# A fused macaron block on one core: scores 12 steps ahead of the exponentials instead of 15, maxima split and loaded at steps 4 and 5 of a unit

## What is computed

```python
x = x + 0.5 * ffn(layernorm(x))
x = x + attn(layernorm(x))
x = x + 0.5 * ffn(layernorm(x))
# ffn(x) = mxfp4(x) @ mxfp4(weight).T + bias: blocks of 32 values are scaled and rounded to 4-bit floats
# attn: q, k, v projections with bias, rotary embedding of q and k, 16 heads of 8 values,
#       softmax(q k^T / sqrt(8)) v over 512 positions
```

## Time and profile before

| | us |
|---|---|
| median of 3 runs | 617.38 |
| lowest and highest | 612.36 and 617.54 |
| the profiled execution | 620.8 |
| its span, first to last instruction | 618.9 |
| mean granted TensorE clock | 0.944 |

### The profile page before, as it was taken

How to read it: one execution, slowest core, us unless ns; L and a number is a source line. 1 busy time by engine, 2 the same in 40 slices (tenths; PEclk the granted TensorE clock), 3 DMA queues, 4 the chain that set the end, 5 groups by cost and what they waited for, 6 DMA issues and landing times.

```text
span 618.9 us, 10478 instructions
## 1 busy us (share of the span) xinstructions
PE 517.9 (84%) x2724; PEld 177.0 (29%) x2724; DVE 452.4 (73%) x1037; ACT 393.2 (64%) x773; POOL 250.7 (41%) x452
## 2 busy tenths in 40 slices
PE   0453999799979998999889897999889995999862
PEld 0121233233323332333223232333323331322211
DVE  6674879587988797768957598869957784788214
ACT  8343149386958684678837585768747683667750
POOL 6010266215753665345723465346723543011300
PEclk9999999799999998899979899999969996999995
DMA  5016102600161015100350015100440026000000
GB/s 159 1 34 143 27 3 53 153 2 1 35 146 27 20 36 128 45 19 11 92 107 19 6 35 131 44 18 19 96 96 19 2 59 147 13 9 1 6 14 17
DMA packets 21685, 30.84 MB, mean 50 GB/s; under 512 B 4333, under 2 KB 19321, under 8 KB 19321
## 3 DMA queue, kind: packets, MB, share of 16 engines
q1 hardware_dynamic: 21624, 30.13, 20.3%
HBM read 21.34 MB, written 8.39 MB: 48 GB/s over the span
## 4 chain that ended last, share of the span: by engine, by line
PE 54%; DMA 11%; DVE 9%; POOL 8%; issue 7%; ACT 6%; SPq 4%; POOLq 0%; ACTq 0%; DVEq 0%
PE sc L1120 15%; PE ot L1133 14%; PE st L1109 12%; DMA feat_k<-parts_k 8%; PE misc L1074 4%; DMA parts_k<-qkparts_k 3%; SPq L333 3%; DVE negmax L908 2%; ACT probs L639 2%; PE misc L1055 2%; PE misc L1098 2%; POOL rstd_f L404 2%; SPq L335 1%; PE misc L1073 1%; POOL qkparts_k L496 1%
## 5 line engine op out<-in xcount | busy, mean ns | idle before, releaser
L908 DVE TENSOR_REDUCE negmax<-sc 128x1 f32<-128x512 f32 x512 | 331.9, 681 | 106.6 <-PE sc L1120 106.2
L639 ACT ACTIVATE probs<-st 128x512 f32<-128x512 f32 x512 | 273.4, 606 | 127.1 <-PE st L1109 126.4
L1120 PE MATMUL sc<-feat_k,feat_q 96*128 96x512 bf16 x512 | 197.8, 411 | 38.6 <-DMA feat_k<-parts_k 23.9
L1109 PE MATMUL st<-feat_q,feat_k 99*128 99x512 bf16 x512 | 162.1, 395 | 2.9 <-ACT probs L639 2.2
L1133 PE MATMUL ot<-probs,vfeat 128*32 128x512 f32 x1024 | 143.2, 634 | 1.0 <-ACT probs L639 1.0
L1120 PEld LDWEIGHTS sc<-feat_k,feat_q 96*128 96x128 bf16 x512 | 51.2, 100 | 208.7 <-DVE negmax L908 127.4
L1109 PEld LDWEIGHTS st<-feat_q,feat_k 99*128 99x128 bf16 x512 | 50.7, 100 | 71.2 <-ACT probs L639 38.8
L467 POOL TENSOR_TENSOR cosd<-qkv,rope 128x256 f32<-128x256 f32 x28 | 20.4, 728 | 57.6 <-ACT qkv L602 57.5
L404 POOL TENSOR_TENSOR rstd_pj<-ve_pj,nhalf 128x4 f32<-128x4 f32 x8 | 8.3, 1038 | 75.2 <-DVE nm_pj L779 75.2
L446 POOL TENSOR_SCALAR maxparts<-negmax 128x16 bf16<-128x16 f32 x32 | 8.3, 258 | 67.9 <-DVE negmax L908 67.9
L1040 PE MATMUL misc<-identb,xq_f 128*128 128x128 bf16 x64 | 6.9, 236 | 28.9 <-DVE xq_f L842 28.3
(11 more groups left out here) (143 smaller groups left out, 529.0 us busy)
## 6 DMA issues: line engine op xcount, KB each, us to landing
feat_q<-parts_q SPq DMA_DIRECT2D x48, 192.0 KB
feat_k<-parts_k SPq DMA_DIRECT2D x48, 192.0 KB
parts_q<-qkparts_q SPq DMA_DIRECT2D x24, 128.0 KB, 2.3
parts_k<-qkparts_k SPq DMA_DIRECT2D x24, 128.0 KB, 2.3
xres<-in_L_attn_x_dram SPq DMA_DIRECT2D x8, 256.0 KB, 5.1
out_dram<-xres SPq DMA_DIRECT2D x8, 256.0 KB, 2.3
feat_q<-maxrows SPq DMA_DIRECT2D x32, 12.0 KB
wload<-in_L_ffn_weight_dram SPq DMA_DIRECT2D x1, 64.0 KB, 2.4
```

The lines of the kernel that those rows point to most:

```text
L639: nc.scalar.activation(probs[:, s % US, j * S:(j + 1) * S], st[:, bank(2 * s + j), :], ACT.Exp, scale=SCALE).then_inc(exp_done, 1)
L908: nc.vector.tensor_reduce(negmax[:, g, j:j + 1], sc[:, bank(16 * g + j), :], AX.X, ALU.max, negate=True).then_inc(sc_maxed, 1)
L1109: nc.tensor.matmul(st[:, bank(2 * s + j), :], feat["k"][par][0:MROWS, h, kb * P:(kb + 1) * P], feat["q"][par][0:MROWS, h, :], start=True, ...
L1120: nc.tensor.matmul(sc[:, bank(16 * g + j), :], feat["q"][par][0:SROWS, h, t * P:(t + 1) * P], feat["k"][par][0:SROWS, h, :], start=True, s ...
```

## The change

The look-ahead of the scores falls from 15 steps to 12. The maxima of a unit then end at step 3 of the unit before, and the split, transposition, copy and load move from steps 1 and 2 to steps 4 and 5 of a unit (steps 4, 12, 20, 28 and 5, 13, 21, 29 of a slot). Nothing else is edited; the number of instructions is the same.

```diff
-LEAD = 15
+LEAD = 12
...
-MAX = dict(split=1, turn=2, copy=2, load=2)
+MAX = dict(split=4, turn=5, copy=5, load=5)
```

## The result

The changed kernel takes 702.37 us in the median of 4 runs (698.94 to 705.91), the kernel before 617.46 (612.36 to 617.68, with one run more than in the table). The ratio is 1.140, 95% interval 1.131 to 1.148: slower, as forecast, by 85 us where 73 had been forecast, inside the range of 665 to 710. The profiled execution took 698.94 us, its span is 697.1. Ratios leave out slow runs, which matters once: a run of 804 us in experiment 7, whose mean granted clock is 0.653 where the other three have 0.938 to 0.947.

What follows compares the result with a forecast made beforehand. No engine is full; PE, nearest, has an in-order queue, so its waits go into the time. 620.8 + 63.7 + 7 + 2 - 2.6 + 3 = 693.9, less 3.4, about 690 us; range 665 to 710.

Steps and rivals of the forecast that it cites:

- Part 1: Step 17, slots 0 to 6: scores move to step 20 and stop waiting for features, at most 19.3 us saved.
- Part 2: Step 16: max rows land 16.6 us after the feature load begins (F); 63.7 us lost, Part 1 included.
- Rival (a): Step 16: only SP's issue holds the max rows, landing at F + 11.1 (F: feature load begins); 649 us, chance 0.12.
- Part 3: Step 13 turn: PE stalls 5.3 us behind POOL's rounding, costing nothing while PE waits later at step 16.
- Parts 4 and 5: Turns: step 5 stalls 1.5 us in slots 0 to 6, taken as 7; steps 21 and 29 add 2.
- Part 6: Kernel ends: three fewer score steps at the start save 3.1 us, the tail adds 0.5; sum -2.6.
- Part 7: TensorE's clock falls to 1.2 GHz after the long stall at step 16 in every slot: +3 us.
- Rival (b): Stalls lower the clock before step 16 and for the whole unit after: 28 us more, 718 us, chance 0.12.
- Rival (c): Step 16: step 13's max rows and turns come in time, features' wait gone, ends shorter: 595 us, chance 0.02.

Runs made afterwards that it cites:

- experiment 7: Changed kernel with 28 extra, unused score matmuls ahead of PE's wait at step 16 of slots 0 to 6: 690.16 us, ratio 1.109.
- experiment 1: Changed kernel with the look-ahead back at 15, the steps of the maxima left at 4 and 5: 707.12 us, ratio 1.139.
- experiment 2: Changed kernel with the feature load one step later, behind the max rows in SP's queue: 630.15 us, ratio 1.018.
- experiment 3: Changed kernel with the second six feature loads one step later, so the max rows stand behind six loads: 636.82 us, ratio 1.028.
- experiment 5: Changed kernel with the first feed-forward's rounding one step later, behind the split on POOL: 705.76 us, ratio 1.138.
- experiment 9: Changed kernel with feature load and rounding each one step later: 602.68 us; with the fourth tile's rotary later too, 603.66; instead with outputs' normalisation earlier, 593.06.

## Why the prediction was right, and which term was too small

**Part 1, the features' wait goes.** Right: one wait of 4.2 us is left. But in this kernel the look-ahead is not needed for it, since PE comes so late: with look-ahead 15 it is gone too (experiment 1). Where PE comes in time, look-ahead 12 takes it away, all but 2.2 us (experiment 2).

**Part 2, the max rows behind the feature load.** Right in place, cause and size. Issue F + 8.1 forecast, F + 8.2 measured; landing F + 16.6 forecast, PE released at F + 16.7 in slot 3, and at F + 16.2 to F + 16.9 over the seven slots; seven waits. They are shorter than the 8 us forecast (6.2 in the mean of slots 0 to 5, 11.9 in slot 6), since PE came to them later. Experiment 2 shows that SP's order decides it, and experiment 3 that the bytes ahead hold it and not the issue alone. Rival (a), 649 us with a landing at F + 11.1, falls with that.

**Part 3, the stall at step 13.** Right: 5.1 us, six times, hidden (experiment 5), and in the open as soon as the rows are in time (experiment 9 against 2).

**Parts 4 and 5, the other turns.** The waits are there: at step 5 1.32 us in slot 3 (1.5 forecast), and behind `turn_out` in the shared bank 6.4 us in 17, at 0.38 each, which less the 4.3 us of the old places is the +2 that was forecast. But they don't show in the balance. From F to F the slots took (508.81 - 108.66) / 6 = 66.7 us before; after, the first and the last are 

```profile
105.39 0.81 SPq L333 DMA_DIRECT2D feat_q<-parts_q  x1
```

```profile
578.54 0.80 SPq L333 DMA_DIRECT2D feat_q<-parts_q  x1
```

(578.54 - 105.39) / 6 = 78.9. The stretch from F to the scores of step 17 takes 10.1 us before and 22.3 after in the mean of slots 0 to 5; without it that leaves 56.6 and 56.5: all of the loss is in that stretch, and parts 4 and 5, +9 in the forecast, were given back elsewhere. One place where they may have been: the scores waited 12.1 us for reductions before, and 2.6 after.

**Part 6, the ends.** Right for the start: F of slot 0 came 108.66 - 105.39 = 3.3 us earlier, 3.1 forecast. The first transposed score, which I had said would come 3 us earlier too, came 83.91 - 79.57 = 4.3 earlier. I had priced a reduction at 0.6 us, where the row has 681 ns.

**Part 7, the clock.** This is the term that was mis-sized, "+3 us". The stretch from step 16's transposed scores to step 17 took 5.8 us and not the 3.4 that I had taken from rows at 2.4 GHz, 2.4 us in each of slots 0 to 5; in slot 6 it took 3.3 and not 1.7: about 16 us in all. Experiment 7 took 9 to 19 us back by keeping PE at work in the wait. Rival (b), whose mechanism this is in part, was right that the clock would come down, and behind the stall at step 13 too; it was wrong that it would stay down for the unit: it was back some 6 us behind the long stall.

**The sum.** Forecast for the profiled execution 693.9, measured 698.94, 5.0 more. Two errors of opposite sign are in that. From F to the scores of step 17 the seven slots lost 82.8 us where the forecast, clock included, had 70.4: 12.4 too little, about what the clock's term lacks (16 against 3). The rest of the kernel came out 4.7 us shorter than before where the forecast had it 2.7 longer: 7.4 too much, the turns above all. That the total is as near as it is owes something to luck. What remains between 690 and the median of 702.37 is how a single execution stands to the median: the one of before was 3.4 us above its median and I took that off, the one of after was 3.4 below.

**Rival (c), faster,** needed the rows of step 13 in time. With that and the rounding repaired, the shift is indeed faster (602.68), and the place that I named decides it. As the change stood, SP's order ruled it out.

## What to carry to other kernels

A step that is moved in a list of steps is moved past every other entry of each queue that it stands in. Here a 12 KB load went from just ahead of twelve 192 KB loads to just behind them, and one place in SP's queue gave 72 us back (702.37 to 630.15), 16 of them the lower clock behind the long wait. Look for the moved item in each engine's queue, DMA queues included, before pricing anything else. A stall that ends in a longer wait has no price of its own yet: the same repair was worth 0 us before the longer wait was gone, and 27 us after.

## What was not expected

A queue of its own did not free the small transfer: 12 KB on ScalarE's queue took 7.3 us from issue to release beside the feature loads, against 8.5 us from issue (350.60) to release behind all twelve on SP's and 5.8 behind six. Its gain went with leaving earlier.

Added matmuls made the kernel faster: 28 of them, 6.2 us of PE time in each of seven slots inside a wait, kept the clock at 2.4 GHz in the four slots where they left 1.1 us of it or less, and took 9 us or more off 702.
